# Whole-bank scores and row maxima, masks by TensorE, and value products in four batches per head group

## The reference

```python
mod = (silu(c) @ wmod)                       # shifts, scales, gates per batch
h = layernorm(x) * (1 + ca) + sa
q, k, v = split(h @ W_qkv.T + b_qkv)         # 16 heads of 16
scores = einsum('bhqd,bhkd->bhqk', q, k) / 4 # causal: keys after the query get -inf
O = softmax(scores) @ v
x = x + ga * (O @ W_o.T + b_o)
h = layernorm(x) * (1 + cb) + sb
# router: top 2 of 8 experts for each token, softmax over the two
y = sum over the two experts e of weight * (silu(h @ w1[e]) @ w2[e])
x = x + gb * y
```

## Time and profile before

| | |
|---|---|
| three runs | 997.82, 999.07, 1000.85 us; median 999.07 us |
| span of the profiled execution, first to last instruction | 997.7 us |
| the profiled execution's own time | taken as its span, 997.7 us; the lowest run lies 0.1 us and the median 1.4 us above it |
| busy: TensorE, VectorE, ScalarE, GpSimd | 902.3, 718.0, 580.5, 357.4 us |
| mean granted TensorE clock | 0.970 of 2.4 GHz |
| attention groups | from 36 to 702 us |
| expert tiles and the end | from 702 us |

### The profile page before, as it was taken

How to read it: one execution, slowest core, us unless ns; L and a number is a source line. 1 busy time by engine, 2 the same in 40 slices (tenths; PEclk the granted TensorE clock), 3 DMA queues, 4 the chain that set the end, 5 groups by cost and what they waited for, 6 DMA issues and landing times.

```text
span 997.7 us, 19445 instructions
## 1 busy us (share of the span) xinstructions
PE 902.3 (90%) x6174; PEld 531.5 (53%) x6174; DVE 718.0 (72%) x2323; ACT 580.5 (58%) x1271; POOL 357.4 (36%) x311
## 2 busy tenths in 40 slices
PE   5899899999899998999999897878899999999990
PEld 3543335433444443543443452423699899999980
DVE  8688766879656789757689669699638584444587
ACT  3335485776585777577666757567535433334562
POOL 1332020431321314333033454015386466565630
PEclk7899899999999999999999999999999999999995
DMA  8446436336326167251662745215313323222699
GB/s 282 127 65 129 61 81 144 59 44 146 63 35 133 42 112 142 69 76 59 106 115 85 152 64 189 73 27 174 96 53 123 95 70 106 78 75 71 198 309 306
DMA packets 83235, 110.61 MB, mean 111 GB/s; under 512 B 15930, under 2 KB 56434, under 8 KB 83138
## 3 DMA queue, kind: packets, MB, share of 16 engines
q1 hardware_dynamic: 75506, 89.45, 38.8%
q0 software_dynamic: 6816, 18.62, 6.1%
q10 hardware_dynamic: 816, 1.32, 0.4%
HBM read 69.42 MB, written 35.41 MB: 105 GB/s over the span
## 4 chain that ended last, share of the span: by engine, by line
PE 62%; DVE 16%; ACT 9%; issue 5%; DMA 4%; POOL 3%; SPq 1%; ACTq 0%; POOLq 0%; DVEq 0%
PE PO L1643 10%; PE PH L1520 9%; PE PY L1520 9%; PE PS L1623 8%; PE PM L1600 8%; ACT PR L1009 4%; DVE MXF L1322 3%; PE PHT L1728 3%; PE PX L1655 2%; PE PX L1569 2%; DVE JK L1319 2%; PE PS L1627 2%; PE PX L1578 2%; PE PX L1579 1%; ACT SF L992 1%
## 5 line engine op out<-in xcount | busy, mean ns | idle before, releaser
L1009 ACT ACTIVATE PR<-PS 128x512 f32<-128x512 f32 (+3 forms) x768 | 334.3, 497 | 142.4 <-PE PS L1627 108.1
L1319 DVE CUSTOM_DVE_ANT_0 JK<-PM,MK 128x128 bf16<-128x128 f32 (+3 forms) x512 | 239.1, 484 | 54.0 <-PE PM L1600 52.8
L1600 PE MATMUL PM<-QK 128*128 128x512 bf16 (+3 forms) x768 | 249.1, 333 | 23.4 <-DVE MXF L1322 15.0
L1623 PE MATMUL PS<-QK 128*128 128x512 bf16 (+3 forms) x768 | 247.5, 333 | 10.4 <-ACT PR L1009 7.4
L1322 DVE TENSOR_REDUCE MXF<-PM 128x1 f32<-128x512 f32 x256 | 175.1, 684 | 83.2 <-PE PM L1600 81.6
L1623 PEld LDWEIGHTS PS<-QK 128*128 128x128 bf16 x768 | 75.0, 98 | 170.4 <-ACT PR L1009 107.8
L1643 PE MATMUL PO<-PR,V 128*17 128x512 f32 (+3 forms) x1536 | 162.8, 496 | 0.0
L1600 PEld LDWEIGHTS PM<-QK 128*128 128x128 bf16 x768 | 75.5, 99 | 98.0 <-DVE MXF L1322 36.8
L1520 PE MATMUL PY<-W2S,HT 128*128 x852 | 118.9, 289 | 2.8 <-issue 1.9
L1520 PE MATMUL PH<-W1S,XT 128*128 x426 | 113.3, 402 | 0.9 <-DVE W2S L1474 0.9
L1627 PE MATMUL PS<-MT,identb 128*128 128x128 bf16 x512 | 111.9, 221 | 0.0
(11 more groups left out here) (269 smaller groups left out, 1194.9 us busy)
## 6 DMA issues: line engine op xcount, KB each, us to landing
QK<-SD SPq DMA_DIRECT2D x180, 128.0 KB
SD<-SP SPq DMA_DIRECT2D x42, 256.0 KB, 2.8
OP<-OS SPq DMA_DIRECT2D x64, 64.0 KB
LP<-LR SPq DMA_DIRECT2D x64, 64.0 KB
W1S<-in_w SPq DMA_DIRECT2D x8, 512.0 KB, 5.7
X<-XA SPq DMA_DIRECT2D x3, 1024.0 KB, 8.8
H2D<-XA SPq DMA_DIRECT2D x3, 1024.0 KB, 4.9
YG<-YT SPq DMA_DIRECT2D x12, 256.0 KB, 4.4
```

What stands on the lines that cost most here:

```text
L1009: eng.activation(PR[:, slot, i, c0:512], PS[m % 3][:, c0:512], ACT.Exp, scale=0.25).then_inc(S["exp"].sem, 1)
L1319: eng.tensor_tensor_reduce(JK[:, jk % 2, 0:w], PM[m % 3][:, 0:w], MK[:, 512 - w:512], 1.0, -3.0e38, ALU.add, ALU.max, MXA[:, mb, h, qt:qt ...
L1600: eng.matmul(PM[m % 3][:, 0:128 * (k1 - k0)], QK[:, r, h, 0, qt * 128:(qt + 1) * 128], QK[:, r, h, 1, k0 * 128:k1 * 128], start=True, stop ...
L1623: last = eng.matmul(PS[m % 3][:, c0:512], QK[:, r, h, 1, j * 128:(j + 1) * 128], QK[:, r, h, 0, 512 * f + c0:512 * f + 512], start=True, s ...
```

## The change

- **Maxima.** `MAXES` replaces the two lists; 38 banks instead of 48, each a tuple (part, query tile, first head, heads, first key tile, width). For every query tile one bank holds the diagonal blocks of all four heads (8 banks of 4 x 128 columns); TensorE first writes the mask for all four (one matmul `identb` x `MK`, 512 columns) and then adds the four products of 128 columns. Query tiles 4 to 7 have four more full banks of 512 (16 in all). The remaining keys below the diagonal are packed: four heads of 128 columns, two of 256 or one of 384 (14 banks). VectorE does a `tensor_reduce` over [128, heads, keys] in every case, into `MX`, which has three parts that start at -3.0e38; the first `cmax` operation reduces over the parts. `tensor_tensor_reduce` is gone.
- **Scores.** 18 slots of two full banks instead of 24. "all" slots are as before; an "odd" slot packs 384 columns of key tile 4f+1 with 128 of 4f+3; a "two" slot packs two heads of key tile 4f+2. Mask matmuls: 8 of 128 columns and 12 of 256 instead of 32 of 128. ScalarE always handles 512 columns.
- **Order.** Banks are spread evenly over the 48 half places of a group (`half_of`).
- **Products.** Four batches a group: key tiles 0 to 3 of the first half; 0 and 1, 2 and 3, and 4 to 7 of the second; each as soon as `LAG` places have passed since its last slot. The matmuls themselves and their widths are the same 48.
- **Ring.** `SLOTS` = 8. The three further slots lie in `PRB`; the memory for them comes from `dynamic_dma_scratch_size=4096` at the creation of the program, where no value was given before.
- At the start: a mask of 512 columns (`MK`) and one of 256 (`MT`) instead of 128 each on GpSimd, one more memset (`MX`) on VectorE.

```diff
-SLOTS = 5
+SLOTS = 8
+FIRST_SLOTS = 5
@@
 def maxima_of(tiles):
-    blocks = []
-    for h in range(4):
-        for q in tiles:
-            blocks += [(h, q, 0, 4, False), (h, q, 4, q + 1, True)] if q >= 4 else [(h, q, 0, q + 1, True)]
-    return blocks
+    banks = []
+    for q in tiles:
+        banks.append((0, q, 0, 4, q, 1))
+        if q >= 4:
+            banks += [(1, q, h, 1, 0, 4) for h in range(4)]
+        if q % 4:
+            heads = (0, 4, 2, 1)[q % 4]
+            banks += [(2, q, h, heads, q // 4 * 4, q % 4) for h in range(0, 4, heads)]
+    return banks
+MAXES = maxima_of(range(4)) + maxima_of(range(4, 8))
@@
-SCORES = [(f, j, p) for f in range(2) for j in range(4 * f + 4) for p in range(2)]
+SCORES = [slot for f in range(2) for slot in
+          [("all", f, j, p) for j in range(4 * f + 1) for p in range(2)] + [("odd", f, 1, p) for p in range(2)] + [("two", f, 2, 0)]]
+BATCHES = ((0, 5, (0, 1, 2, 3)), (5, 9, (0, 1)), (9, 13, (2, 3)), (13, 18, (4, 5, 6, 7)))
+def score_pieces(n, i):
+    kind, f, j, p = SCORES[n]
+    if kind == "all":
+        return [(2 * p + i, j, 0, 512, 0)]
+    if kind == "odd":
+        return [(2 * p + i, 4 * f + 1, 128, 512, 128), (2 * p + i, 4 * f + 3, 0, 128, 384)]
+    return [(2 * i, 4 * f + 2, 0, 256, 256), (2 * i + 1, 4 * f + 2, 256, 512, 256)]
+def half_of(name, n):
+    return n * 2 * NW // (NM if name == "max" else 2 * NS)
@@ ScalarE, score
-                    if m // 2 >= SLOTS:
-                        ac.wait_ge(S["pv"], (m // 2 - SLOTS) // 2 + 1)
-                    eng.activation(PR[:, slot, i, c0:512], PS[m % 3][:, c0:512], ACT.Exp, scale=0.25).then_inc(S["exp"].sem, 1)
+                    if s >= SLOTS:
+                        ac.wait_ge(*after("pv", "pv", (s - SLOTS) // NS, batch_of((s - SLOTS) % NS)))
+                    eng.activation(PR[s % SLOTS][:, i, :], PS[m % 3][:, :], ACT.Exp, scale=0.25).then_inc(S["exp"].sem, 1)
@@ VectorE, max
-                    if diag:
...
-                        eng.tensor_tensor_reduce(JK[:, jk % 2, 0:w], PM[m % 3][:, 0:w], MK[:, 512 - w:512], 1.0, -3.0e38,
-                                                 ALU.add, ALU.max, MXA[:, mb, h, qt:qt + 1]).then_inc(S["mx"].sem, 1)
-                    else:
-                        eng.tensor_reduce(MXF[:, mb, h, qt - 4:qt - 3], PM[m % 3][:, 0:w], AX.X, ALU.max).then_inc(S["mx"].sem, 1)
+                    eng.tensor_reduce(MX[:, g % 2, part, h:h + heads, q],
+                                      PM[m % 3][:, 0:128 * heads * width].rearrange("p (h k) -> p h k", h=heads), AX.X,
+                                      ALU.max).then_inc(S["mx"].sem, 1)
@@ TensorE, max
-                    eng.matmul(PM[m % 3][:, 0:128 * (k1 - k0)], QK[:, r, h, 0, qt * 128:(qt + 1) * 128],
-                               QK[:, r, h, 1, k0 * 128:k1 * 128], start=True, stop=True).then_inc(S["m"].sem, 1)
+                    if part == 0:
+                        eng.matmul(PM[m % 3][:, :], identb[:, :], MK[:, :], start=True, stop=True)
+                    for i in range(heads):
+                        last = eng.matmul(PM[m % 3][:, 128 * width * i:128 * width * (i + 1)],
+                                          QK[:, r, h0 + i, 0, q * 128:(q + 1) * 128],
+                                          QK[:, r, h0 + i, 1, k0 * 128:(k0 + width) * 128], start=part > 0, stop=True,
+                                          skip_group_check=True)
@@ TensorE, pv
-                    g, f, j = a
-                    pe.wait_ge(*after("exp", "score", g, n, 1))
+                    g, b = a
+                    n0, n1, keys = BATCHES[b]
+                    pe.wait_ge(*after("exp", "score", g, n1 - 1, 1))
+                    for j in keys:
+                        for h in range(4):
+                            n, i, c0, c1, q0 = place_of(f, j, h)
+                            last = eng.matmul(PO[32 * h:32 * h + 17, q0:q0 + c1 - c0], V[g // 4 % 2][:, j, 4 * (g % 4) + h, :],
...
-    nc = bacc.Bacc("TRN2", target_bir_lowering=False, num_devices=1)
+    nc = bacc.Bacc("TRN2", target_bir_lowering=False, num_devices=1, dynamic_dma_scratch_size=4096)
```

More of the change, by code:

```diff
@@ L217, in schedule @@
         for f, n in ((2, NM),) if g else ((0, NM0), (1, NM)):
[L218 removed]
+            place(g, end_of(n) - LEAD - (f == 0), [(0.5 if g and i else 0, ("cmax", g, f, i)) for i in range(6)]
                   + [(CROW if g else 1 if f == 0 else 2, ("crow", g, f))])
         if g == 0:
[L221 removed]
+            place(0, end_of(NM0) - LEAD + 3, one("rep", 1, 2))
@@ L222, in schedule @@
         if g < NG - 1:
             place(g + 1, LAG + 1, one("od", g))
-        for n, (f, j, p) in enumerate(SCORES):
-            if p == 1:
-                place(g, n + LAG - ahead(g, f), one("pv", g, f, j))
+        for n, (_, f, _, _) in enumerate(SCORES):
+            k = half_of("score", 2 * n + 1) // 2 - ahead(g, f)
+            b = batch_of(n)
+            if n == BATCHES[b][1] - 1:
+                place(g, k + LAG, one("pv", g, b))
+    max_at = {half_of("max", n): n for n in range(NM)}
@@ L312 @@
 NR = len(ROUTE[0])
-LATE = ()
 RING = 10
```

185 lines of the change are left out of this document (97 added, 88 removed).

## The result

The changed kernel takes 1009.03 us in the median of four runs (1007.63 to 1016.9), the kernel before took 998.92 beside it: a ratio of 1.012, with a 95% interval of 1.008 to 1.016. It is 10 us slower. The forecast was 1001.2 us with a range of 986 to 1016, so the time lies in the range, but the likeliest case, an even trade, is not what happened. The profiled run is the one of 1007.63 us, with a span of 1005.6 us, 7.9 more than before.

What follows compares the result with a forecast made beforehand. It took TensorE to bound eight attention groups and VectorE seven. Terms +0.6 (TensorE's groups), 0 (VectorE's) and +1.5 (last group) gave +2.1 us on the profiled 997.7, 999.8; with the median 1.4 above, 1001.2 us, range 986 to 1016.

Steps and rivals of the forecast that it cites:

- an even trade: Attention on TensorE: masks cost what batches give, +0.08 us a group; likeliest case, chance 0.44, 0.25 of it within 0.3%.
- Prices on TensorE: TensorE: 0.055 us per 128 columns in full stream, 0.213 us per 128 product columns, 0.23 us fixed per step.
- the rival of the weight loads: Maxima on TensorE: narrow matmuls need their weight load, 1.8 us a group, +14 us, 1018 us; chance 0.05.
- Parts 1 and 3: TensorE, each group: maxima masks add 1.76 us; batches save eight fixed parts, 1.68 us.
- Part 4: VectorE's maxima: 22.7 us a group become 22.1, saving 0.6 us, at most 4.0.
- The rings: Rival: uniform banks and fewer hand-overs between engines remove waits, -14 us, 987 us; chance 0.28.
- Part 6: Longer product blocks: VectorE dry 3.2 us a group at full banks; nothing in TensorE's groups, 0.6 us in VectorE's seven.
- the rival of the starved VectorE: Long blocks starve VectorE where it rules: up to 2.6 us a group, +18 us, 1017 us; half 1010; chance 0.18.
- Its own sign: In the groups where VectorE rules: VectorE idle behind `PM` for over 1 us after most batches.
- Part 5: ScalarE's exponentials: 12 of 48 instructions fall away, at most 2.0 us a group; counted nothing because of slack.
- Part 7: ScalarE: slot waits are over when scores arrive; the `PO` copy delays exponentials 0.5 us, covered by three free banks.
- Part 8: End of group 15: a four-tile batch of 2.36 us replaces a 0.35 us step, +1.5 us, bounds 0 and +2.

Runs made afterwards that it cites:

- half reduces: Changed kernel, each maxima reduce reading half its columns, exponentials' scale a tenth: 983.14 us with four batches, 984.03 us with ten steps.
- ten steps: Changed kernel with its products in ten steps a group, of one or two key tiles, instead of four batches: 1004.33 us, ratio 1.002.
- the shorter scratch alone: Kernel before with dynamic_dma_scratch_size=4096 and nothing else changed: 1002.73 us, ratio 1.001.
- maxima alone: Changed kernel with the unpacked scores and twelve product steps of before, keeping new maxima, eight slots and shorter scratch: 1003.68 us, ratio 1.002.
- the old maxima: Changed kernel with the 48 blocks and masked custom operations of before, keeping packed scores and four batches: 1036.58 us, ratio 1.035.

## Why the prediction came out as it did

**Prices on TensorE: right.** A diagonal bank of group 10, on TensorE's timeline:

```profile
487.75 0.38 PE L1648 MATMUL PM<-MK,identb 128*128 128x512 bf16 x1
487.96 0.39 PE L1650 MATMUL PM<-QK 128*128 128x128 bf16 x4
488.19 0.38 PE L1677 MATMUL PS<-QK 128*128 128x512 bf16 x1
```

From the mask to the next score it is 0.44 us, as forecast; four products of 128 columns with four weights take 0.23, so narrow matmuls keep the full pace, and the rival of the weight loads is gone. The batch of four key tiles takes 2.28 us from its first start to the next instruction, and ten tiles of 128 columns x 0.213 are 2.13: only the way out, 0.15, is left, with nothing at the passages between key tiles. A switch avoided is worth 0.17 us (half reduces, quiet groups) where 0.21 was taken.

**The number.** The time lies in the range because the range was wide enough to take in half of a rival that had 0.18; the account that had the most weight gave +2.1 us, and +10.1 was measured, outside even its slower cases (up to +9). So that the range holds is no proof of the account.

**Parts 1 and 3, the even trade: nearly right, in the quiet groups.** Masks +1.76 (1.5 measured by leaving them out, 1.2 by adding them alone), eight switches -8 x 0.17 = -1.4 for -1.68. Group 10 went from 36.4 to 37.2 us by its first exponentials, under the 1 us that would have made all of it wrong; groups 2, 6 and 10 went up by 0.6 us each in the mean, where 0.08 stood with bounds up to +0.6. In the eight groups together the change is +2.4 us for +0.6. But there both sides of the trade are smaller than taken: leaving out the masks brings 6.0 us of 14.1, and six switches bring 3.0 us (half reduces) where 8 x 6 x 0.21 = 10 would stand. That the trade stays even outside the quiet groups is luck: TensorE's work was taken to count in full in all eight, and it doesn't.

**Part 4, VectorE: right.** Full banks are 0.60 us apart, outputs add nothing. The records' sum fell from 464.5 us (422.6 and 41.9 of accumulator reads) to 398.1, 4.1 us a group, which is what the upper bound of 4.0 was made of, and none of it is seen as time. The rings did not loosen: the two lines of waits for VectorE stayed at 53 to 56 us.

**Part 6, longer blocks: this step failed.** It said that in TensorE's groups a batch "costs nothing, since VectorE can spare 11 us", and gave 0.6 us to each of VectorE's groups. The mistake is to hold an average against a ring of three banks. It also took TensorE to ask for a bank every 0.5 us, which would carry six places; it asks every 0.43 us, and the fifth waits. What the runs show in its place is read from four batches against ten steps, with full and with half reduces (us by which four batches are longer, sums over groups, from one profile of each kernel):

```
                 2,3,5,6,7,9,10,11    0,1,4,8,12    13,14     15
full reduces          +0.8              +5.5        +2.0     +2.0
half reduces          -3.0              -1.3        +6.9     +2.8
difference             3.8               6.8
```

The difference is what VectorE's pace makes of the batches: 0.5 us in each of TensorE's eight groups where Part 6 had nothing, 1.4 us in each of five of VectorE's where it had 0.6. Groups 13 and 14 can't be used, for the clock, and group 15 has no maxima. Over the run it turns six saved switches into 10 us lost.

So the rival of the starved VectorE had the better account, with 0.18: it named VectorE's groups and up to 2.6 us in each, and half its price, 1010 us, lies next to the measured 1009, in part by chance, since against the kernel before its seven groups are only 3.8 us longer. Its own sign came: of the 27 batches in its seven groups, 17 have VectorE idle in front of a bank for over 1 us. In these groups VectorE's idle time before its maxima is 67.0 us, 60.3 in ten steps, and the groups are 7.5 us longer; in TensorE's eight it is 95.9 for 88.0, and they are 0.8 longer, since there the switches saved pay for most of it. Not every batch does it. In group 4 VectorE stays busy all through one that TensorE starts at 241.50 and that takes 2.5 us:

```profile
241.59 1.25 DVE L1368 TENSOR_REDUCE MX<-PM 128x4 f32<-128x512 f32 x2
242.76 0.42 DVE L1304 BATCH_NORM_STATS2 BNS<-XA 128x6 f32<-128x256 f32 x1
243.21 0.18 DVE L1306 BATCH_NORM_AGGREGATE MV<-BNS 128x2 f32<-128x6 f32 x1
243.31 0.66 DVE L1368 TENSOR_REDUCE MX<-PM 128x1 f32<-128x512 f32 x1
```

Against the kernel before none of this is seen in VectorE's groups: 4, 8 and 12 stayed at 42.2 us for 42.1 (ten steps: 41.2), and 0, 1, 4, 8 and 12 together at 225.3 for 225.2. Part of the reason is that the kernel before has 10.2 us at the lower clock in groups 0 and 1, worth up to 5 us.

**Part 5, ScalarE: mostly right.** Nothing shows where TensorE rules. But it said that without the slack the fewer exponentials would be a gain, and group 15 is that case: 26.9 becomes 24.4 us in ten steps. Four batches give it back as idle time of ScalarE.

**Part 7, waits moved: incomplete.** It counted the 0.5 us of the copy of `PO` and not ScalarE's wait for the batch in front of it, 53.8 us in all. In the quiet groups that costs nothing that shows, in group 15 it does.

**Part 8, ends: right in size.** From the last exponential to the first expert tile 3.6 us became 5.3, +1.7 for +1.5.

**After 702 us** nothing was to change, and in the one profile the experts' part takes 1.7 us more. Of these, 1.4 us lie between the fourth and the fifth tile, where the changed kernel ran at the lower clock (722.6 to 726.0) and the one before at the upper; the fourth tile's six products, before and after:

```profile
716.68 1.55 PE L1520 MATMUL PH<-W1S,XT 128*128 x6
722.80 2.76 PE L1567 MATMUL PH<-W1S,XT 128*128 x6
```

From the first tile's product to the end, 292.2 us before and 293.9 after, the profiles of the shorter scratch alone and of ten steps have 296.9 and 298.0 with the same experts' code, so this stretch moves by itself. The missing 8 us of the forecast (+10.1 measured beside +2.1) are thus about 4 us more in the attention, 1.7 in this stretch, and the rest within what single profiles and medians differ by.

What stays open: how much of groups 13 and 14 is the clock's. They are longer in ten steps than with maxima alone (49.6 and 45.6 us for group 13), with 10.2 and 3.4 us at the lower clock, which can account for up to 3.4 of the 4.0 us; what sends the clock down was not tested. Open too is how the loss on the old maxima gets as large as 27 us over the new, of which the clock can be up to 19. A version that beats both kernels was not found; ten steps are level with the kernel before.

## What to carry to other kernels

An engine's slack over a stage says nothing of what a long block of another engine costs it. Hold the length of the block against what the ring between them holds in time (here three banks of 0.6 us, and steps of 1.0 us left the kernel level with before while those of 1.9 did not), and count what is filled when the block begins. Where the consumer sets the pace, its idle time behind the block is the kernel's time; where it has time to spare, it still costs some.

An edit that costs time alone (packed scores, 0.7%) need not cost it beside another, so price edits together. Read the granted clock of a stretch before you explain why it is longer. And before work is moved out of one engine's queue, look for whose input then stands behind it.

## What the runs showed of the hardware

Key tiles of the narrow products follow each other without any loss (ten tiles of 0.213 us in 2.28), while a change from the full array to the four narrow tiles and back costs 0.23 us by the earlier trace rows and 0.17 us as measured by leaving six out (half reduces, quiet groups); it pays to batch them only where nobody is fed by the work between. Four bf16 products of 128 columns, each with new weights, take 0.23 us. A reduce of 512 columns costs 683, 684 and 687 ns with one, two and four outputs. At TensorE's lower clock a product step takes 1.84 us for 0.99, and six products with expert weights 2.76 for 1.55.
